# Five tiles of experts 0 to 2 placed among the ranking of the last batches

## The reference

```python
# B=8 batches of S=256 tokens, D=512; 8 experts, 192 wide, top 2
def _L0_xattn_ref(hidden_states, memory_tokens, memory_mask):
    scores = jnp.einsum('bsd,bmd->bsm', hidden_states, memory_tokens) * scale
    scores = jnp.where(memory_mask[:, None, :], scores, neg_inf)
    attn = jax.nn.softmax(scores, axis=-1)
    return jnp.einsum('bsm,bmd->bsd', attn, memory_tokens)   # 0 where a batch has no valid token

def _L0_ffn_ref(x, w_router, w_gate, w_up, w_down):
    probs = jax.nn.softmax(xt @ w_router.T, axis=-1)
    top_v, top_i = jax.lax.top_k(probs, TOP_K)
    top_v = top_v / jnp.sum(top_v, axis=-1, keepdims=True)
    comb = comb.at[jnp.arange(T)[:, None], top_i].add(top_v)
    g = jnp.einsum('th,eih->tei', xt, w_gate)
    u = jnp.einsum('th,eih->tei', xt, w_up)
    act = jax.nn.silu(g) * u
    out = jnp.einsum('tei,ehi,te->th', act, w_down, comb)

x = x + jnp.tanh(g_xattn[0]) * _L0_xattn_ref(_layernorm(x, axis=-1), ctx_2048, mask_BxS2_bk0)
x = x + jnp.tanh(g_ffn[0]) * _L0_ffn_ref(_layernorm(x, axis=-1), w_router, w_gate, w_up, w_down)
```

## Time and profile before

| | |
|---|---|
| median of 3 runs | 274.59 us (273.13 to 275.19) |
| the profiled execution | 275.0 us |
| its span, from the first to the last instruction | 273.1 us |
| PE busy | 248.7 us (91%) |
| DVE busy | 173.9 us (64%) |
| ACT busy | 145.9 us (53%) |
| POOL busy | 154.3 us (56%) |
| mean granted TensorE clock | 0.976 |

### The profile page before, as it was taken

One profiled execution on the slowest core, in us unless ns is written; L12 is line 12 of the kernel. 1 busy time (PEld: TensorE's weight loads), 2 busy tenths in 40 slices (PEclk: granted clock), 3 DMA queues, 4 the chain that ended last, 5 costly groups with the idle time before them and its releaser, 6 DMA issues.

```text
span 273.1 us, 5968 instructions
## 1 busy us (share of the span) xinstructions
PE 248.7 (91%) x1672; PEld 222.8 (82%) x1672; DVE 173.9 (64%) x605; ACT 145.9 (53%) x326; POOL 154.3 (56%) x175
## 2 busy tenths in 40 slices
PE   8999999999999887899999998998999999999600
PEld 8898997889888767799999997897999999999500
DVE  4466899998998997166666665565566544444300
ACT  3456757657675623256656664655556554445300
POOL 3355558577674332526828558658578488483820
PEclk9999999999999999999999999999999999999955
DMA  5996998999997231786778988848859778587670
GB/s 175 364 373 216 349 301 292 306 301 312 327 287 241 102 134 48 218 317 107 173 229 127 184 233 160 176 94 174 160 100 162 146 114 168 114 160 150 97 99 0
DMA packets 30625, 53.18 MB, mean 195 GB/s; under 512 B 5312, under 2 KB 9536, under 8 KB 30592
## 3 DMA queue, kind: packets, MB, share of 16 engines
q0 software_dynamic: 8304, 19.83, 39.2%
q1 hardware_dynamic: 22288, 32.94, 36.1%
HBM read 33.81 MB, written 18.95 MB: 193 GB/s over the span
## 4 chain that ended last, share of the span: by engine, by line
PE 64%; DVE 14%; issue 6%; DMA 5%; ACT 4%; POOL 2%; SPq 1%; POOLq 0%; ACTq 0%
PE S L1137 8%; PE S L1138 8%; PE S L1141 8%; PE PV L1013 6%; PE S L1000 6%; PE A L1127 5%; DMA XG<-x2s,IXI 4%; PE PC L1023 3%; DVE st L670 3%; PE PV L1160 3%; PE PV L1161 3%; PE PV L1165 3%; PE PV L1162 3%; PE PV L1164 3%; DVE TB L774 2%
## 5 line engine op out<-in xcount | busy, mean ns | idle before, releaser
L486 POOL DMA_INDIRECT out<-YT,IXI x36 | 58.3, 1620 | 45.6 <-issue 20.2
L1137 PE MATMUL S<-WGh,XTh 128*128 x144 | 51.5, 358 | 0.2 <-ACT XTh L601 0.2
L461 POOL DMA_INDIRECT XG<-x2s,IXI x39 | 39.5, 1013 | 16.8 <-issue 10.4
L1138 PE MATMUL S<-WGl,XTh 128*128 x144 | 48.5, 337 | 0.0
L622 ACT ACTIVATE YT<-PV,cj 128x512 f32<-128x512 f32 x36 | 24.8, 690 | 22.1 <-PE PV L1165 22.1
L917 DVE TENSOR_TENSOR XTl<-A,XTh 128x512 fp32r<-128x512 f32 x37 | 25.6, 692 | 14.7 <-ACT XTh L601 14.7
L1013 PE MATMUL PV<-CX,PT 128*128 128x260 f32 x128 | 31.6, 390 | 1.4 <-ACT PT L530 1.4
L405 POOL TENSOR_TENSOR rs<-mv,CS 128x1 f32<-128x1 f32 x32 | 18.2, 568 | 24.3 <-DVE mv L676 24.0
L608 ACT ACTIVATE SG<-S 128x192 f32<-128x192 f32 x36 | 11.9, 331 | 37.0 <-PE S L1141 37.0
L1000 PE MATMUL S<-CT,XLT 128*128 128x264 f32 x128 | 31.1, 386 | 0.0
L1141 PE MATMUL S<-WGh,XTl 128*128 x144 | 30.9, 337 | 0.0
(11 more groups left out here) (144 smaller groups left out, 521.1 us busy)
## 6 DMA issues: line engine op xcount, KB each, us to landing
WGl<-in_wgu SPq DMA_DIRECT2D x24, 256.0 KB, 5.8
X<-in_x SPq DMA_DIRECT2D x16, 256.0 KB, 4.7
CT<-in_ctxt SPq DMA_DIRECT2D x8, 512.0 KB, 6.0
CX<-in_ctxn SPq DMA_DIRECT2D x8, 512.0 KB, 5.8
out<-X SPq DMA_DIRECT2D x16, 256.0 KB, 4.4
x2s<-Y SPq DMA_DIRECT2D x16, 256.0 KB, 4.3
WD1l<-in_wd SPq DMA_DIRECT2D x8, 256.0 KB, 6.0
WS<-in_wd SPq DMA_DIRECT2D x8, 256.0 KB, 5.6
```

The costliest lines, as they stand in the source:

```text
L461: pool.indirect_dma_start(out=XG[:, j % NX, :], out_offset=None, in_=x2s, in_offset=bass.IndirectOffsetOnAxis(ap=IXI[:, j:j + 1], axis=0))\
L486: pool.indirect_dma_start(out=out, out_offset=bass.IndirectOffsetOnAxis(ap=IXI[:, j:j + 1], axis=0), in_=YT[:, j % NB, :], in_offset=None, ...
L1137: pe.matmul(o, XTh[:, j % 2, c, :], WGh[:, bass.ds(e, 1), c, :], start=(c == 0), stop=False)
L1138: pe.matmul(o, XTh[:, j % 2, c, :], WGl[:, bass.ds(e, 1), c, :], start=False, stop=False)
```

## The change

Five tiles, two of expert 0, two of expert 1 and one of expert 2 (`EARLY`), become tiles 0 to 4. Their rows are taken from the table of batches 0 to 4 (`RB` is 5): after `tab(4)` DVE copies the bank, one small matmul (`IXE`) picks the five columns, DVE writes their token numbers, and POOL gathers them while batches 5 to 7 are ranked. The tiles themselves are written between the ranking steps of the last batches on PE, DVE, ACT and POOL; they all use the banks A0, A1 and PO. The filler matmuls of that stretch go. The 40 tiles of the selection come after them (`NR`), with ranks less by the tiles already taken (`FIRST`). If a tile of the five isn't full with rows of batches 0 to 4, the ranks of later batches move up to the next tile (`cne`, added to `Rn`). The weight splits keep their order, three tiles later by number (`SHIFT`). The weight of the second expert is taken by Tanh in place of Exp and a reciprocal (`half_gap`, `coefs`). POOL makes the five coefficients itself (`coef`), and its order is written out: gathers 0 to 4 among `ln2` of the last half batches, then scatters and gathers by hand up to gather 9. Scatters 2, 4 and 5 always wait for all before them. SP's later weight loads wait for gather 5 in place of gather 1. Rows of padding move to the front of `x2s` and `out` (`OFF`).

```diff
+EARLY = [(0, 0), (0, 1), (1, 0), (1, 1), (2, 0)]
+NE = len(EARLY)
+NR = 40
+NT = NE + 39
+NTP = NE + NR
...
+SHIFT = 3
+FIRST = [sum(e == f for f, _ in EARLY) for e in range(E)]
...
-RB = 6
+RB = 5
...
+        def xbank(j):
+            return A0 if j < NE else (A0, A1)[(j - NE) % 2]
...
-            sp.wait_ge(s_g[1], 16)
+            sp.wait_ge(s_g[NE], 16)
...
+            for s in range(STEPS - 5):
...
+                known = x2s[0:OFF + RB * S, :] if j < NE else x2s
                 if j >= NX:
...
+            def scatter(j):
+                pool.wait_ge(s_y, j + 1)
+                if j > NE:
+                    fence(j)
+                elif j == NE or j and EARLY[j][0] != EARLY[j - 1][0]:
+                    landed(j)
+                pool.indirect_dma_start(out=out, out_offset=bass.IndirectOffsetOnAxis(ap=IXI[:, j:j + 1], axis=0),
+                                        in_=YT[:, j % NB, :], in_offset=None, compute_op=ALU.add)\
...
+            def coef(j):
+                pool.wait_ge(s_g[j], 16)
+                if j >= 4:
+                    pool.wait_ge(s_y, j - 3)
+                pool.tensor_scalar(cj[:, j % 4:j % 4 + 1], XG[:, j, D + EARLY[j][0]:D + EARLY[j][0] + 1],
+                                   GB[:, 8:9], 1.0, ALU.mult, ALU.mult).then_inc(s_cj, 1)
...
+            pool.wait_ge(s_ixi, 1)
+            pool.wait_ge(s_sc, NTK)
+            pool.wait_ge(s_cwp, B)
+            pool.wait_ge(s_zd, 32 * NPAD)
+            pool.wait_ge(s_sy[0], 16 * RB)
+            pool.wait_ge(s_sy[1], 16 * RB)
+            pool.wait_ge(s_scb[0], 16 * RB)
+            for j in range(3):
                 gather(j)
+            ln2(NTK - 2)
+            for j in range(3, NE):
+                gather(j)
+            ln2(NTK - 1)
+            for j in range(4):
+                coef(j)
+            for k in range(8, NTK):
+                pool.wait_ge(*stored(k))
+            scatter(0)
+            for j in range(4, NE):
+                coef(j)
+            scatter(1)
+            pool.wait_ge(s_ixi, 2)
+            pool.wait_ge(s_sy[0], 16 * 8)
+            pool.wait_ge(s_sy[1], 16 * 8)
+            pool.wait_ge(s_scb[1], 16 * (B - RB))
+            gather(NE)
+            gather(NE + 1)
+            scatter(2)
+            gather(NE + 2)
+            gather(NE + 3)
+            scatter(3)
+            gather(NE + 4)
             pool.wait_ge(s_tn, 1)
             turns = [pool.value_load(TN[0:1, g:g + 1], min_val=0, max_val=(1 << 13) - 1) for g in range(3)]
             live = tiles_of(pool)
-            for j in range(NT):
+            for j in range(4, NT):
                 with lives(pool, live, j):
-                    pool.wait_ge(s_y, j + 1)
...
+                for i in range(2):
+                    act.activation(e2[:, i, :], dd[:, i, :], ACT.Tanh, scale=rs2[:, 2 * b + i:2 * b + i + 1])\
+                        .then_inc(s_e2, 1)
...
+            x2ln(NTK - 2)
+            for k in range(9, 13):
+                act.wait_ge(*stored(k))
+            silu(0)
+            xhi(1)
+            half_gap(B - 1)
+            hhi(0)
+            x2ln(NTK - 1)
+            for j in range(1, NE):
+                silu(j)
+                xhi(j + 1)
+                if j == 3:
+                    act.wait_ge(s_sy[0], 16 * 8)
+                    act.wait_ge(s_sy[1], 16 * 8)
+                yev(j - 1)
+                hhi(j)
+                if j >= SHIFT:
+                    hi(PRE + j - SHIFT)
+                if j == 3:
+                    rows()
             live, crowd = tiles_of(act), crowded(act)
...
+                    dve.tensor_tensor(cne[:, :], lim, CNE, ALU.subtract).then_inc(s_cr, 1)
+                    yield
+                    dve.wait_ge(s_cr, b + 1)
+                    dve.scalar_tensor_tensor(out=Rn[:, :], in0=cne[:, :], scalar=0.0, in1=Rf[:, :],
+                                             op0=ALU.max, op1=ALU.add).then_inc(s_rn, 1)
+                    yield
...
                 dve.wait_ge(s_e2, 2 * b + 2)
-                n = mark(dve.tensor_scalar(den[:, :, :], e2[:, :, :], 1.0, None, ALU.add))
-                yield
-                need(n)
-                n = mark(dve.reciprocal(cc[:, :, 0:1], den[:, :, :]))
-                yield
-                need(n)
-                n = mark(dve.tensor_tensor(cc[:, :, 1:2], cc[:, :, 0:1], e2[:, :, :], ALU.mult))
+                dve.tensor_scalar(cc[:, :, 0:1], e2[:, :, :], -0.5, 0.5, ALU.mult, ALU.add)
+                yield
+                n = mark(dve.tensor_scalar(cc[:, :, 1:2], e2[:, :, :], 0.5, 0.5, ALU.mult, ALU.add))
...
+            def index(src, p, q):
+                link(dve.scalar_tensor_tensor(out=zz[:, 0:q - p], in0=src, scalar=0.0, in1=padr[:, p:q],
...
+            dve.wait_ge(s_tab, RB)
+            dve.tensor_copy(Tsb[:, :], PTB[:, 0:128]).then_inc(s_tse, 1)
+            run(braid(x2(NTK - 3), top2(B - 2)))
+            dve.wait_ge(s_ixe, 1)
+            index(IXE, 0, NE)
+            run(rowmax(NTK - 1), ranks(B - 2), gap(B - 2), hits(B - 3), norm(NTK - 1))
+            run(braid(x2(NTK - 2), slots(B - 2)), coefs(B - 2))
+            last = x2(NTK - 1)
+            next(last)
+            run(top2(B - 1), ranks(B - 1))
             xlo(0)
+            next(last)
+            run(braid(slots(B - 1), queue(last, gap(B - 1))))
+            for k in range(9, 13):
+                dve.wait_ge(*stored(k))
+            dve.wait_ge(s_y2, 13)
+            mul(0)
+            xlo(1)
+            run(hits(B - 2))
+            hlo(0)
+            run(heads(B - 1))
+            mul(1)
+            xlo(2)
+            run(braid(hits(B - 1), coefs(B - 1)))
+            hlo(1)
+            mul(2)
+            run(tiles())
+            dve.wait_ge(s_tab, B)
...
+                if s == NTK:
+                    pe.wait_ge(s_tse, 1)
+                    pe.wait_ge(s_cr, B - 2)
+                    pe.wait_ge(s_cw, B)
+                    pe.matmul(IXE, Tsb[:, :], pick, start=True, stop=True).then_inc(s_ixe, 1)
...
+            def counts():
+                cum(B - 1)
...
+                pe.wait_ge(s_cr, B)
+                pe.wait_ge(s_sel, 2)
+                pe.matmul(ERP, eq, sel[:, :], start=True, stop=True)
+                pe.matmul(IXR, Tsb[:, :], sel[:, :], start=True, stop=True).then_inc(s_ixp, 1)
+
+            def owners():
...
+                pe.matmul(PL[:, 0:NR * E], onesb, selE[:, :, :].rearrange("p j e -> p (j e)"), start=True, stop=True)\
+                    .then_inc(s_ejp, 1)
...
             tx(0)
-            warm(10)
-            own, live = {0: expert(0)}, None
-            for j in range(NT):
+            pe.wait_ge(s_xw, NTK)
+            warm(8)
+            gu(0, first(0), counts)
+            tx(1)
+            th(0)
+            gu(1, first(1))
+            tx(2)
+            tab(B - 2)
+            down(0, first(0))
+            th(1)
+            gu(2, first(2))
+            tx(3)
+            tab(B - 1)
+            down(1, first(1))
+            th(2)
+            gu(3, first(3), index)
+            tx(4)
+            down(2, first(2))
+            th(3)
+            owners()
+            gu(4, first(4))
+            pe.wait_ge(s_er, 1)
+            own, live = {j: first(j) for j in range(NE)}, None
+            own[NE] = bass.ds(expert(NE), 1)
+            tx(NE)
+            down(3, first(3))
+            th(4)
+            pe.wait_ge(s_ixi, 2)
+            for j in range(NE, NT):
                 with lives(pe, live, j):
                     if j in [due(e) for e in range(PRE // 5, E)]:
-                        pe.wait_ge(s_wd, j - 1)
```

380 lines of the change are left out of this document (208 added, 172 removed).

## The result

The changed kernel takes 286.85 us in the median of 4 runs (285.46 to 289.05), the kernel before 274.33 us on the same chip; the ratio is 1.0467, 95% interval 1.0389 to 1.0545. It is slower by 12.5 us where 8.6 us less were predicted. The profiled execution has a span of 284.8 us, 11.7 more than before.

What follows compares the result with a forecast made beforehand. Ranking and filler before tile 0, then PE's pace with late gathers, were taken to bound the kernel. 275.0 - 10.7 (earlier tiles) + 0.5 + 0.1 (small terms) + 1.5 (fences) = 266.4 us, range 261.5 to 271.5.

Steps and rivals of the forecast that it cites:

- What bounds the kernel: Ranking and filler before tile 0, then PE's pace of 3.91 us a tile, with 2.5 us lost to late gathers.
- Part 1: Start of the tiles: transposes of tile 0 at 98.9 instead of 111.06, 12.2 us earlier.
- Part 2: Pace of tiles 0 to 4: 1.5 us of added matmuls; gate matmuls of tile 5 at 121.0, 10.7 us gained.
- the rival of DVE's order: Early tiles: DVE's order sets their pace, 4 us more, 270.4 us; chance 0.07.
- Part 3: Small terms: register loads before tile 5 0.5 us, longer constants' load 0.1, loop and end 0.
- Part 4: POOL's fences, more and sooner: later gathers after tile 5 give 1.5 us back.
- New lateness 4.0: PE's lateness from late gathers after tile 5: 4.0 us (2.0 to 4.5) in place of 2.5.
- The one on the other side, fences at 8.7: Fenced scatters: spacing 8.7 us everywhere, gathers of 6.9, 17.5 us late, 279.9 us; chance 0.05.
- The clock's rival: PE without filler: clock falls to 1.2 GHz, three tiles at 3.9 us more each, 278.1 us; chance 0.04.
- Gathers all in time: Gathers: POOL keeps ahead, so the earlier 2.5 us of lateness go as well, 261.8 us; chance 0.10.
- the chance of slower, 0.08: Whole kernel: chance of a slower result, from the dearest fences and the clock, some 0.01 from mixed cases.
- the rule that the prediction weighed: PE's waits for gathers: by the rule every burst starts at the lower clock, giving 278.1 rather than 266.4 us.

Runs made afterwards that it cites:

- e7_loop: Changed kernel with room for 39 tiles, plus empty steps ahead of the coefficients and one-hot tables in DVE's order; 275.11 us (kernel before in its group 280.1).
- e5_spread: Changed kernel with room for 39 tiles, the last 19 weight loads issued about one for each tile instead of in bursts; 272.92 us, ratio 0.9775.
- e8_nofence: Changed kernel with room for 39 tiles, each tile's scatter to its own DRAM tensor, so no fences; 266.45 us in one run (kernel before 280.1).
- e10_before_same: Kernel before plus empty steps in DVE's order and one late weight load for each tile; 280.42 us, ratio 0.9979.
- e9_all: Changed kernel with room for 39 tiles, empty DVE steps, spread weight loads and expert 2 first after the early tiles; 266.85 us, ratio 0.9506.
- e13_room41: Changed kernel with room for 41 tiles instead of 44, so 5 bodies are stepped over; 282.25 us, ratio 1.0232.
- e6_order: Changed kernel with room for 39 tiles, expert 2 first after the early tiles and no fence at tile 5; 273.83 us, ratio 0.9786.

## Why the prediction was wrong

**What bounds the kernel** was read rightly: filler and ranking left the path, and 12.84 us of the 13.42 went.

**Part 1** holds. The prediction has tx(0) 1.3 us behind the last x2; it is 0.58, with PE waiting 0.9 for the gather, behind which the 1.0 us counted for register loads does not show. With the loop mended tx(0) is at 98.46 (e7_loop) where 98.9 was said.

**Part 2** holds: tx(0) to tx(5) took 2.3 us more than before, with the register loads, where 2.0 were counted. DVE fits in; the rival of DVE's order, 4 us more, is out.

**Part 3 failed in two sentences.** "cc by Tanh has one DVE instruction fewer for each batch ... both lie beside PE in the loop: 0" put the loop at nothing, and it cost 4.26 us. It priced the instruction and not its place: what counted was which instruction met POOL's split. PE is busy in the loop, but DVE was on its path. The coefficients alone account for 1.3 to 1.4 us of it; the rest was lost in the steps with tables, by DVE's order too (e7_loop has it back), but what set that off is open. And "The end, from the last eviction on, is the same work" left out the end's 9.21 us: 6.8 in PE's hole ahead of the last down, about 1 for the clock behind it, 1.4 from the last scatter on. Part 3 had just found that 36 tiles remain; that the code now has bodies for 44, eight of them to be passed at the end, was in the diff, and the sum had no term for it. The 0.77 us of tx(20) to tx(36) were missed as well; with room for 39 this stretch is 62.42 again. Twelve tiles after load a second register, seven before.

**Part 4** had the mechanism and mis-sized it. A fenced spacing away from loads was said to be 6.2 and is 5.54 (scatter 4 to 5); the two scatters from 5 to 7 take 9.6, where 9.4 were said. But the loads were laid at 135.0, behind scatter 4; that is the second group. The first, of eight, waits for gather 5 in place of gather 1, so it moved from 113 to 124.02, onto scatter 3: 9.04 us and not 6.2. Then "New lateness 4.0" counted waits alone. PE waited 5.8 us (4.01, 1.00, 0.43 and 0.35); of the fences' 9.5 us another 1.6 are the step at the lower clock behind gather 15 (5.54 - 3.9), and the remaining 2.1 lie in other steps. The net is 7.63 in place of 1.5. e5_spread and e8_nofence show both parts.

**The rivals.** The one on the other side, fences at 8.7, had the right direction for this stretch, and its price came once, beside the loads. The clock's rival came in small: not three tiles at 3.9 us each but one step that cost 1.6, behind the one long wait, and 0.9 us for the last down. A whole tile at the lower level was seen once, tile 0 of e10_before_same: 5.71 us against 3.59 in the kernel before, so 2.1 more and not 3.9. Two sums of the prediction do not come out, without bearing on the outcome: "Gathers all in time" leaves out the 0.6 us of part 3 (it would be 262.4), and the chance of slower, 0.08, is less than the 0.05 and 0.04 of its two rivals together. On the rule that the prediction weighed (the Trainium skill, TensorE: Matmul & The Clock Gate, "HAM oscillation — how this bites in real kernels": waits between bursts let the clock fall) the rows show both: 0.68 behind the 4.01 us, 1.00 behind the 1.00 us at 150.15. No tile was short: 36 scatters.

That e9_all lands at 266.85, near the 266.4, is luck and no confirmation: it has one fence fewer and spread loads.

## What to carry to other kernels

A change that moves work ahead also changes what meets what: look at every shared place where the moved or removed instruction stood (here DVE beside POOL's splits, SP's wait beside a fence), and price what stands behind an instruction that is held, not the instruction. Room for cases that do not occur is paid for where the code is passed over: count the bodies that are not run between the last work and the end. And a late transfer can cost more than the wait: behind the longest one the next step ran at a lower clock.

## What the runs showed of the hardware that was not expected

Passing code that is not run cost PE 1.24 us for each body of 23 matmuls from 5 to 8 bodies, and one branch over all eight spared only 1.0 us. The length of a wait alone did not decide the clock behind it: 0.69 from 152.0 to 157.5 in e13_room41, behind 1.83 us, and 1.00 from 176.2 to 180.3 in e6_order, behind 2.53. A DVE instruction on two columns took 1.25 us beside a POOL split, seven times its 0.17. In e10_before_same something held up the 84 fillers ahead of tile 0. PE's timeline has

```profile
114.19 0.39 PE L973 MATMUL S<-CB 128*128 128x128 bf16 x4 [1.01 <-issue]
...
115.63 0.38 PE L973 MATMUL S<-CB 128*128 128x128 bf16 x4 [1.05 <-issue]
...
117.24 0.63 PE L1131 MATMUL A<-CS,XG 128*128 128x128 f32 x2
```

groups of four fillers with a microsecond of "issue" between them, and tile 0 came 8.8 us behind its gather's start where 4.04 was shown before. The granted clock was below 1.00 as well, 0.74 from 106 to 112 and 0.52 in the step of tile 0, which took 5.71 us (117.24 to 122.95) where the kernel before took 3.59. The kernel before, with the same fillers, took 280 to 282 us at the lower mean clock in this and two other groups, and 275 in two. That the fillers are the reason in those runs was not tried, and no trace shows it.
